# Second gate of a graph kernel: queries copied by TensorE as three bf16 parts

## What is computed

```python
h = relu(rgcn(x, W_rel1, W_root1, b1));  h = gate(h, query_embs, Wg, bg, Wq, bq)
h = relu(rgcn(h, W_rel2, W_root2, b2));  h = gate(h, query_embs, Wg, bg, Wq, bq)

def gate(h, q, Wg, bg, Wq, bq):      # 8 batches, 8 nodes and 64 queries each, 768 features
    hg = h @ Wg[:, :F].T             # per node
    qg = q @ Wg[:, F:].T + bg        # per query
    attn = sigmoid(hg[:, :, None, :] + qg[:, None, :, :])
    qi = einsum('bnlf,blf->bnf', attn, q)
    alpha = sigmoid(h @ Wq[:, :F].T + qi @ Wq[:, F:].T + bq)
    return alpha * tanh(qi) + (1 - alpha) * h
```

## Time and profile before

| | |
|---|---|
| median of 3 runs | 266.50 us (266.43 to 267.36) |
| the profiled execution's own time | 266.77 us |
| its span in the profile | 264.7 us |
| busy: PE, DVE, ACT, POOL | 247.8, 155.2, 89.1, 84.2 us |
| granted TensorE clock | 1.00 in every stage of the change, 0.996 mean |
| DMA | 53.46 MB, 202 GB/s mean |

### The profile page before, as it was taken

How to read it: one execution, slowest core, us unless ns; L and a number is a source line. 1 busy time by engine, 2 the same in 40 slices (tenths; PEclk the granted TensorE clock), 3 DMA queues, 4 the chain that set the end, 5 groups by cost and what they waited for, 6 DMA issues and landing times.

```text
span 264.7 us, 4922 instructions
## 1 busy us (share of the span) xinstructions
PE 247.8 (94%) x2037; PEld 127.2 (48%) x2037; DVE 155.2 (59%) x280; ACT 89.1 (34%) x151; POOL 84.2 (32%) x78
## 2 busy tenths in 40 slices
PE   8899999997999999899999998899998988999994
PEld 4675654443545542367765222225563443445572
DVE  0845322617887999841027999995667367405322
ACT  2323210008676995320003576770302013013000
POOL 7581000006997799300001778770000000000000
PEclk9999999999999999999999999999999999999998
DMA  7999999899802969200999910005999545000001
GB/s 237 373 401 399 401 315 154 140 354 404 313 1 45 402 268 355 9 0 15 271 408 401 402 58 2 0 2 142 395 403 402 208 143 217 0 0 2 0 2 30
DMA packets 39911, 53.46 MB, mean 202 GB/s; under 512 B 22985, under 2 KB 23753, under 8 KB 39890
## 3 DMA queue, kind: packets, MB, share of 16 engines
q1 hardware_dynamic: 29792, 51.64, 54.9%
q10 hardware_dynamic: 10098, 1.52, 3.5%
HBM read 52.17 MB, written 0.20 MB: 198 GB/s over the span
## 4 chain that ended last, share of the span: by engine, by line
PE 65%; POOL 10%; DVE 9%; ACT 6%; issue 5%; DMA 4%; SPq 1%; DVEq 0%; POOLq 0%
PE ps L1142 12%; PE ps L1258 11%; PE ps L1110 10%; POOL prod L621 6%; POOL W L621 4%; PE ps L1157 4%; DMA W<-in_L_gnn_Wg 4%; PE ps L1536 3%; PE ps L1347 3%; PE ps L1616 3%; PE ps L1227 3%; PE ps L1086 3%; ACT pre L702 2%; PE ps L1404 2%; DVE prod L912 2%
## 5 line engine op out<-in xcount | busy, mean ns | idle before, releaser
L621 POOL TENSOR_TENSOR prod<-pre,qn 128x768 f32<-128x768 f32 x28 | 54.3, 1955 | 12.5 <-ACT pre L702 12.5
L920 DVE TENSOR_TENSOR pre<-ps,qg 128x768 f32<-128x768 f32 x46 | 43.1, 950 | 6.3 <-PE ps L1404 3.4
L702 ACT ACTIVATE pre<-pre 128x768 f32<-128x768 f32 x46 | 38.5, 848 | 5.5 <-DVE pre L920 5.0
L1258 PE MATMUL ps<-W 128*128 128x384 f32 x96 | 35.2, 492 | 0.7 <-ACT W L458 0.4
L458 ACT COPY W<-ps 128x384 f32<-128x384 f32 x35 | 16.0, 482 | 24.9 <-PE ps L1086 24.7
L702 ACT ACTIVATE ps<-ps 128x768 f32<-128x768 f32 x18 | 14.2, 794 | 29.6 <-PE ps L1333 21.4
L1347 PE MATMUL ps<-prod,rsel 128*32 128x384 f32 x192 | 20.5, 497 | 1.8 <-POOL prod L621 1.0
L1258 PEld LDWEIGHTS ps<-W 128*128 128x128 f32 x96 | 17.1, 190 | 10.3 <-issue 2.2
L1142 PE MATMUL ps<-W,prod 128*64 128x256 f32 (+1 forms) x240 | 20.6, 328 | 0.0
L1142 PEld LDWEIGHTS ps<-W,prod 128*64 128x64 f32 x240 | 15.1, 137 | 4.9 <-issue 0.5
L1086 PE MATMUL ps<-ident,W 128*128 128x128 f32 x108 | 16.7, 282 | 0.8 <-DMA W<-in_L_gnn_Wg 0.4
(11 more groups left out here) (244 smaller groups left out, 336.6 us busy)
## 6 DMA issues: line engine op xcount, KB each, us to landing
W<-in_L_gnn_W SPq DMA_DIRECT2D x9, 2304.0 KB, 12.8
W<-in_L_gnn_W_rel SPq DMA_DIRECT2D x6, 2304.0 KB, 17.3
W<-in_L_gnn_W_root SPq DMA_DIRECT2D x2, 2304.0 KB, 16.4
W<-in_L_gnn_Wq SPq DMA_DIRECT2D x4, 1152.0 KB, 9.4
qn<-in_L_gnn_query_embs SPq DMA_DIRECT2D x4, 384.0 KB, 10.0
W<-in_L_gnn_Wg SPq DMA_DIRECT2D x3, 384.0 KB, 3.9
W<-in_L_gnn_Wg SPq DMA_DIRECT2D x1, 1152.0 KB, 9.5
W<-in_L_gnn_Wg SPq DMA_DIRECT2D x12, 96.0 KB, 4.0
```

The lines of the kernel that those rows point to most:

```text
L621: nc.gpsimd.tensor_tensor(prod_of(T), pre_of(T), qn[:, pair_and_node(t)[0], :], ALU.mult).then_inc(prod_p, 1)
L702: nc.scalar.activation(tile, tile, ACT.Sigmoid).then_inc(sig_ready, 1)
L920: nc.vector.tensor_tensor(dst, ring(T), by_half(qg[:, pair_and_node(T % TILES)[0], :]), ALU.add).then_inc(pre_ready, 1)
L1258: ins = nc.tensor.matmul(ps[:, unit_bank(u), 0:HD], qT[:, k, p * P:(p + 1) * P], WgT_q[:, k, c * HD:(c + 1) * HD], start=(k == 0), stop=(k ...
```

## The change

All left tiles of the second gate become D, also the seven that were X. The fp32 copy becomes twelve bf16 matmuls: qg is split into three bf16 parts (hi, mid, low) that together carry the fp32 value. The split is done during the second graph layer, after relation 0, in four chunks of 128x768: ScalarE copies to bf16, VectorE subtracts, twice in turn. Instead of `qs` one DMA pair, issued after the first gate, puts the second halves of qg with exchanged rows into `pre[:, 0:2]` (`swapped`); `pre[:, 2:4]` takes the remainders. The parts lie in slot 2. For this rel2_0 and rel2_1 exchange slots, and L2_W1_0 is loaded after the gate, ahead of L2_W1_1. PE waits for the last part (`q_low_ready`) where it waited for `qs`.

```diff
--- before.py
+++ after.py
@@ -39,7 +39,7 @@
 
 
     PLAN = [("Wg_q", 0, 2), ("Wg_h", 4, 6), ("rel1_0", 5, 1), ("rel1_1", 6, 1), ("rel1_2", 0, 1), ("root1", 3, 1),
-            ("Wq_h", 5, 2), ("Wq_q", 6, 2), ("rel2_0", 3, 1), ("rel2_1", 2, 1), ("rel2_2", 5, 1), ("root2", 6, 1),
+            ("Wq_h", 5, 2), ("Wq_q", 6, 2), ("rel2_1", 3, 1), ("rel2_0", 2, 1), ("rel2_2", 5, 1), ("root2", 6, 1),
             ("L1_W", 5, 1), ("L2_W1_0", 2, 1), ("L2_W1_1", 3, 1), ("L2_W1_2", 6, 1),
             ("L2_W2_0", 4, 1), ("L2_W2_1", 0, 1), ("L2_W2_2", 1, 1), ("L3_W1", 5, 1), ("L3_W2", 2, 1)]
     SLOT = {key: s for key, s, _ in PLAN}
@@ -112,7 +112,24 @@
         warm = W[2][:, 0, 0:256].bitcast(BF16)
         qT = W[2][:, :, 0:NP * P]
 
-        qs = W[SLOT["L2_W1_1"]][:, 0:2, :].rearrange("p a (b f) -> p (a b) f", b=2)
+        swapped = pre[:, 0:2, :].rearrange("p a (b f) -> p (a b) f", b=2)
+        rest = pre[:, 2:4, :].rearrange("p a (b f) -> p (a b) f", b=2)
+        splits = W[SLOT["L2_W1_0"]][:, :, :].rearrange("p a b -> p (a b)").bitcast(BF16).rearrange(
+            "p (s c q f) -> p s c q f", s=3, c=2, q=NP)
+        Q_CHUNKS = [(c, q) for c in range(2) for q in range(0, NP, 2)]
+
+        def q_split(part, i):
+            c, q = Q_CHUNKS[i]
+            return splits[:, part, c, q:q + 2, :]
+
+        def q_source(i):
+            c, q = Q_CHUNKS[i]
+            return qg[:, q:q + 2, 0:HD] if c == 0 else swapped[:, q:q + 2, :]
+
+        def q_rest(i):
+
+            c, q = Q_CHUNKS[i]
+            return (rest, swapped)[c][:, q:q + 2, :]
         more_prod = W[SLOT["L2_W1_1"]][:, 2:2 + PRODS, :]
 
         qn_f = qn[:, :, :].rearrange("p a b -> p (a b)")
@@ -213,7 +230,11 @@
         nodeT_ready = sem("nodeT_ready")
         hg_done = sem("hg_done")
         hi_ready = sem("hi_ready")
-        qs_loaded = sem("qs_loaded")
+        swapped_loaded = sem("swapped_loaded")
+        q_hi_ready = sem("q_hi_ready")
+        q_rest_ready = sem("q_rest_ready")
+        q_mid_ready = sem("q_mid_ready")
+        q_low_ready = sem("q_low_ready")
         mid_ready = sem("mid_ready")
         mid_part = sem("mid_part")
         low_ready = sem("low_ready")
@@ -268,7 +289,7 @@
 
         POOL_TILES = [t * 3 // 2 for t in range(20)]
         KINDS = ["P" if t in POOL_TILES else "V" for t in range(TILES)] + list(
-            "DP" "DP" "XP" "DP" "XP" "DP" "XP" "DP" "XP" "DP" "XP" "DP" "XP" "DP" "XX" "DD")
+            "DP" * 14 + "DX" "DD")
         AHEAD = (TILES, TILES + 2)
         IN_SBUF, POOL_MUL = "PV", "P"
         HALF_T = TILES // 2
@@ -511,8 +532,8 @@
             sp.wait_ge(loaded["Wg_h"][BY_BLOCK[-1]], 16 * (P // GN))
             load("Wq_h", Wq[:, 0:D], rgcn_done, 1)
             load("Wq_q", Wq[:, D:2 * D], rgcn_done, 2)
-            load("rel2_0", a["L0_gnn_W_rel2"][0], rgcn_done, R + 1)
-            load("rel2_1", a["L0_gnn_W_rel2"][1], qg_done, UNITS)
+            load("rel2_1", a["L0_gnn_W_rel2"][1], rgcn_done, R + 1)
+            load("rel2_0", a["L0_gnn_W_rel2"][0], qg_done, UNITS)
             load("rel2_2", a["L0_gnn_W_rel2"][2], turned, G_QH + GROUPS)
             load("root2", a["L0_gnn_W_root2"], turned, G_END)
             sp.wait_ge(qk_cleared, 1)
@@ -522,17 +543,17 @@
                 sp.dma_start(qk[:, :, 1, q:q + 1], halves(a[f"L2_gnn_{name}2"]),
                              allow_slow_non_contiguous=True).then_inc(qk_loaded, 16)
             done = R + 1
-            sp.wait_ge(rgcn_done, done + 1)
+            sp.wait_ge(reduced, TILES // 2)
             for c in range(2):
-                sp.dma_start(qs[c * N:(c + 1) * N, :, :],
-                             qg[(1 - c) * N:(2 - c) * N, :, c * HD:(c + 1) * HD]).then_inc(qs_loaded, 16)
-            load("L2_W1_0", a["L2_gnn_W1"][0], rgcn_done, done + 2)
+                sp.dma_start(swapped[c * N:(c + 1) * N, :, :],
+                             qg[(1 - c) * N:(2 - c) * N, :, HD:D]).then_inc(swapped_loaded, 16)
             load("L1_W", a["L1_gnn_W"], rgcn_done, done + 3)
             load("L2_W1_2", a["L2_gnn_W1"][2], rgcn_done, done + 4)
             load("L2_W2_0", a["L2_gnn_W2"][0], hg_done, 2)
             sp.wait_ge(reduced, TILES)
             for c, name in enumerate(("q", "k")):
                 sp.dma_start(qk_rows[c], a[f"L2_gnn_{name}2"].rearrange("f o -> o f").to_broadcast([P, D])).then_inc(qk_rows_loaded, 16)
+            load("L2_W1_0", a["L2_gnn_W1"][0])
             load("L2_W1_1", a["L2_gnn_W1"][1])
             load("L2_W2_1", a["L2_gnn_W2"][1], alpha_done, 4)
             load("L2_W2_2", a["L2_gnn_W2"][2])
@@ -670,6 +691,22 @@
                 mix_copy(layer)
                 if layer == 0:
                     load_blocks(act, 1)
+                else:
+                    act.wait_ge(rgcn_done, R + 2)
+                    act.wait_ge(swapped_loaded, 32)
+
+                    def q_hi(i):
+                        nc.scalar.copy(q_split(0, i), q_source(i)).then_inc(q_hi_ready, 1)
+
+                    def q_mid(i):
+                        act.wait_ge(q_rest_ready, i + 1)
+                        nc.scalar.copy(q_split(1, i), q_rest(i)).then_inc(q_mid_ready, 1)
+
+                    q_hi(0)
+                    for i in range(1, len(Q_CHUNKS)):
+                        q_hi(i)
+                        q_mid(i - 1)
+                    q_mid(len(Q_CHUNKS) - 1)
 
                 for i, (part, ready, stacked) in enumerate(((hi, hi_ready, hi_stacked), (mid, mid_ready, mid_stacked),
                                                             (low, low_ready, low_stacked))):
@@ -863,6 +900,21 @@
                     for k in BY_BLOCK:
                         dve.wait_ge(loaded["Wg_h"][k], 16 * (P // GN))
                         nc.vector.transpose(WgT_h[:, k, :], WgT_h[:, k, :]).then_inc(WgT_h_ready, 1)
+
+                if layer == 1:
+                    def q_take(i):
+                        dve.wait_ge(q_hi_ready, i + 1)
+                        nc.vector.tensor_tensor(q_rest(i), q_source(i), q_split(0, i), ALU.subtract).then_inc(q_rest_ready, 1)
+
+                    def q_low(i):
+                        dve.wait_ge(q_mid_ready, i + 1)
+                        nc.vector.tensor_tensor(q_split(2, i), q_rest(i), q_split(1, i), ALU.subtract).then_inc(q_low_ready, 1)
+
+                    q_take(0)
+                    for i in range(1, len(Q_CHUNKS)):
+                        q_take(i)
+                        q_low(i - 1)
+                    q_low(len(Q_CHUNKS) - 1)
 
                 if layer == 0:
                     dve.wait_ge(rgcn_done, R + 1)
@@ -1314,14 +1366,13 @@
             def copy_queries(T):
 
                 p = pair_and_node(T % TILES)[0]
-                for c in range(2):
-                    rows = slice(c * N, (c + 1) * N)
-                    nc.tensor.matmul(ring(T)[rows, c, :], ident[rows, rows], qg[rows, p, c * HD:(c + 1) * HD],
-                                     start=True, stop=False)
-                for c in range(2):
-                    rows = slice(c * N, (c + 1) * N)
-                    other = slice((1 - c) * N, (2 - c) * N)
-                    nc.tensor.matmul(ring(T)[other, c, :], ident[rows, rows], qs[rows, p, :], start=True, stop=False)
+                for part in range(3):
+                    for c in range(2):
+                        for half in range(2):
+                            rows = slice(half * N, (half + 1) * N)
+                            to = half if c == 0 else 1 - half
+                            nc.tensor.matmul(ring(T)[to * N:(to + 1) * N, c, :], ident_b[rows, rows],
+                                             splits[rows, part, c, p, :], start=(part == 0), stop=False)
 
             def add_nodes_rows(tiles):
 
@@ -1467,7 +1518,7 @@
                     project_wide(nodeT, WgT_h, HG1, (0,), first=False, chunks=BY_BLOCK[3:],
                                  waits={1: (nodeT_ready, 4)}).then_inc(hg_part, 1)
                     project_wide(nodeT, WgT_h, HG1, (1,), first=False).then_inc(hg_done, 1)
-                    pe.wait_ge(qs_loaded, 32)
+                    pe.wait_ge(q_low_ready, len(Q_CHUNKS))
                     for T in AHEAD:
                         copy_queries(T)
                 (first_gate, second_gate)[layer]()
```

## The result

| | before | changed |
|---|---|---|
| median | 266.43 us | 265.29 us |
| ratio, 95% interval | | 0.9962 (0.9951 to 0.9972) |
| span of the profiled execution | 264.7 us | 263.4 us |

The change gains 1.14 us of 266.43, 0.4%. The medians are of six runs each, taken in turn on the same chip.

The account below looks back on a forecast made before the run. VectorE was taken to bound the second gate. With its additions removed, PE's items summed to a last reduction at 169.43 + 15c = 178.43 instead of 179.81, 1.38 us gained, giving 265.1 us; range 263.8 to 268.3 us.

Parts of the forecast that it names:

- The bound: Second gate before the change: VectorE, busy 4.46 of 4.50 us with 40 operations, sets the step of 2.29 us.
- c = 0.60: Each step of the second gate: twelve bf16 matmuls copying queries on PE take 0.60 us, lower bound 0.48.
- The rival in which neighbours wait for each other: Gate copy: matmuls on different rows and one bank can't overlap; copy 1.08 us, total 272.3 us; chance 0.10.
- upper bound of 0.81: Gate copy priced as the fp32 copy with its turn, 0.69 + 0.12 us; total 268.3 us; 0.65 to 0.81 had chance 0.14.
- The sum of the gate: PE's items in the second gate: last reduction starts at 169.43 + 15c = 178.43, before 179.81; 1.38 us gained.
- likeliest case: Gate copy between 0.57 and 0.65 us: gain 0.6 to 1.8 us, total 264.7 to 265.9 us; chance 0.54.
- slope of 0.15 us per 0.01 us of c: Second gate: each 0.01 us of copy time counts in fifteen copies, 0.15 us of the time.
- GpSimd's path: Second gate, a P tile's way from row matmuls to reduction: 5.97 us for three steps, 1.99 each, level with PE.
- The split: Splitting queries in the second graph layer: 8.5 to 9 us, done near 133, hidden by 1.4 us; late: chance 0.05.
- The loads: Weight loads after the gate: L2_W1_1 lands 4.9 us ahead of use, no cost; late, up to 271 us: chance 0.04.
- fixed terms: Items in PE's gate sum beside the copies: warming matmuls 0.54 us, alpha blocks 0.58 each, a reduction 0.79.

Follow-up runs that it names:

- two parts with a lag of three: Changed kernel with the third (low) part of each copy left out, eight bf16 matmuls instead of twelve: 263.94 us, ratio 0.9887.
- of four: Changed kernel with the third part of each copy left out and each reduction four steps behind instead of three: 262.32 us, ratio 0.9846.

## Why the prediction came out as it did

**The bound.** That VectorE set the step before is borne out. It was busy 4.46 of 4.50 us; with its additions kept, cheaper copies gained nothing, and with the additions gone it waits for PE.

**The copy, c = 0.60.** Measured 0.62. The quarters of the array work at once although both 64-row halves write one bank: the copy keeps the pace of the row matmuls. The rival in which neighbours wait for each other (c = 1.08, 272 us) is ruled out. By the rule that the Trainium skill gives in TensorEngine Tiling (Array Packing), section Restrictions and Gotchas, different row tiles cannot access one PSUM bank simultaneously; the trace does not agree, if that is meant for different partitions too: twelve such matmuls, four at a time, took 0.62 us here. The upper bound of 0.81 was the right price of the fp32 copy with its turn, and the kernel that has it was slower than before, 268.24 us: 1.4 us by its ratio and 1.6 in the gate, where the sum gave 1.8.

**The sum of the gate.** It gave k=3 at 150.76 and the last reduction at 178.43 on the old clock. In the profile after k=3 starts at 150.63 and the last reduction at 178.42:

```profile
178.42 0.19 PEld L1398 LDWEIGHTS ps<-W,rsel 128*32 128x32 f32 x8 [0.76 <-DVE W L964]
```

The gate starts 0.16 earlier there (141.95 against the earlier trace rows), so the end is 0.15 later than summed: fifteen copies at 0.01 to 0.02 more. That the two errors cancel, and the last reduction comes within 0.01 us of its forecast, is luck. What was right is the sum: 1.2 us gained in the gate where 1.38 was forecast, and 1.14 between the medians. The likeliest case came true, in the lower half of its gains. The gain is 0.4%, less than the 0.5% that I had taken as what can be told from no change: the forecast of 265.1 us lay just beyond that limit, and the chance of a larger gain (0.45) was put above that of a change within it (0.36). The stated range, 263.8 to 268.3 us, holds the time before as well, so the time alone tested little; the copy, the step and the waits in the trace did. The slope of 0.15 us per 0.01 us of c held too: 0.16 more cost 2.2 us.

**GpSimd's path.** It was said to be level with PE, and to eat part of a cheaper copy. Both are shown, by two parts with a lag of three (a third step of 2.20 us) and of four (1.83 throughout).

**The split.** Forecast to end near 133, ended at 132.03. The copies took 0.83 and the subtractions 0.95, as taken, and from start to start a subtraction occupied 0.87, so the whole took 8.15 us instead of 8.5 to 9. The 1.30 us that twelve products took on average in the first gate did not show here, where GpSimd is idle.

**The loads.** L2_W1_1 lands 16.8 us after its issue at 181.3, at 198.1, and the matmuls that need it start at 203.04:

```profile
L508 SPq DMA_DIRECT2D W<-in_L_gnn_W x2: 436/490/545, 180.9 to 181.3; - x2
...
DMA to landing us min/median/max: 11.4/14.1/16.8
```
```profile
203.04 1.94 PE ps L1587 x12
```

It is 4.9 us early, the margin that was forecast.

**What was missing** is not in the sum but beside it. Warming matmuls and alpha blocks stood in the sum as fixed terms, 0.54 and 0.58 each, and so did a reduction in step 3, 0.79. With the change all three lie on PE's path, while in the kernel before, by its trace, VectorE's work hid most of their time. I wrote them down as costs and did not ask whether they still had to be there. By the gates in the traces the runs found 1.1 us in the first, 0.5 in the second and 0.9 in the lag, 2.5 together. How much of this the kernel before would have given too was not run.

## What to carry to other kernels

When work moves from a bound engine to the next one, add up the next engine's whole step item by item, and give each item its price with the turn to the next shape: here 0.08 us more for the copy in each of fifteen steps would have cost the gain. After such a move look again at everything that was placed in the old bound's waits (filling matmuls, side work, how far a reduction lags): it may now lie on the path. Here taking it out or moving it was worth 2.5 us in the gate, all three together, and the change itself 1.2. A loop has several paths of nearly one length, each through other tiles and buffers; so before you reorder two items, say which wait each of them had covered.

## What the runs showed of the hardware that I had not expected

No row before the change showed this pattern, and the prediction could only give it odds. Bf16 matmuls of 64x64 on the two row halves, which write different partitions of one PSUM bank at the same time, don't hold each other up: twelve of 384 columns in 0.62 us with the turn to the next shape, eight in 0.45 (164.80 to 165.25 above). Two parts and three differ by 0.17 us, one set of four. For comparison, five bf16 matmuls of 512 columns that follow one another take 1.09 us in the changed kernel (L1279, 195.00 to 196.09), 0.22 each; an estimate from this for one of 384 columns is 0.16 us, so the four of a set take about the time of one.
